# A post-norm attention and feed-forward layer: no setup stage, channel-major input, weights prepared during attention, first norms moved ahead

## The chip, the cores and the metric

The kernel runs on one core of a Trainium2 chip. The metric is the device time of one execution in microseconds, lower is better. TensorE (PE) multiplies, VectorE (DVE), ScalarE (ACT) and GpSimd (POOL) work element by element, and SyncE (SP) issues every DMA here. The engines are ordered by semaphores alone, and each works its own list in order.

## The reference

The input x is 8 x 2048 x 256 in float32. Cut to what matters:

```python
q = x @ q_w.T + q_b
xd = conv1d(x, conv_w, stride 2, padding 1, one filter of 3 per channel) + conv_b
k, v = xd @ k_w.T + k_b, xd @ v_w.T + v_b            # 1024 keys for 2048 queries
a = softmax(q k^T / 4) v                              # 16 heads of 16
x = layernorm(x + a @ out_w.T + out_b)
h = layernorm(x) * gamma + beta
w1, w2 = (fc1_q - 128) * scales1, (fc2_q - 128) * scales2    # int32, scales by rows of 128
y = silu(h @ w1 + b1) @ w2 + b2
out = layernorm(x + x + 0.5 * y)
```

## The kernel before, in words

The 16384 rows are 32 blocks of 512, four for each of 8 batches (`QB`, `NB`, `BPB`). Channels are two chunks of 128 partitions (`CC`). Where accuracy needs it, a float32 value is split into an upper and a lower half (`_hi`, `_lo`), the lower made on GpSimd. Products on float32 tiles issue two PE records each (the order's "x4" is eight records in the trace). The program is four stages, each a block in which all engines start together and end together.

**setup** (L127) loads the int32 weights, the scales and biases. DVE and ACT make w1 and w2 from them, DVE and GpSimd the halves (L228 to L244, L188). PE makes the hidden bias (w1 times beta, L208: 16 products of one column) and the output biases (L203, L214, L215). GpSimd also makes the identity and fills the rows of `k_s` that must be one (L183).

**project** (L252) handles one block after another. PE turns the block of x, loaded by rows, into channels: eight transposes (L348) that ACT copies out (L389). DVE does the convolution (L429 to L437). PE makes q (L359), k (L367), v (L374). ACT copies them out with their biases, and DVE and GpSimd make the halves. SP stores q_hi, q_lo, k_hi, k_lo and v to DRAM (`store`, L299) and loads x for the next batch. v is stored with 16 ones beside the 16 channels of each head (`VC` is 32): with them the weighting also yields the softmax's denominator. At b = 7, keys, values and queries of the first head group are loaded (L332, L333) before the last four stores.

**attention** (L467) has 32 blocks of 32 steps: four groups of four heads (`G`, `HG`), in each eight tiles of 128 keys. In step s PE does the scores of step s + 1 (L602), the products whose maxima are wanted 12 steps later (`first`, L577, `LEAD`), and the weighting of step s (`weigh`, L612). DVE takes the maxima (L683), ACT the exponentials (L658). The maxima of a group are turned by PE (L588) in the fourth step of each group, copied by DVE (L697) and put by SP as one more row into `q_s` (`load_max`, L504). The first score of a group waits for that (L595). SP's list (`one_block`, L515) is in order: in each group `load_max` for the next group, then new q, then the store of o (L535). In the last block of a batch it waits for the group's end, loads its keys and values (`load_kv`, L116) and waits for them to land before q:

```python
sp.wait_ge(pv_done, STEPS * n + KT * (g + 1) + 2)
sp.wait_ge(begun, 1)
load_kv(sp, e, next_kv, g)
sp.wait_ge(kv_loaded[g], KVL * (next_kv + 1))
```

That happens 7 x 4 = 28 times. In the last 12 steps of the last block there are no `first` products. The denominators of blocks 0 to 23 are loaded, inverted (L715) and stored there; `rden_d` is read later.

**finish** (L718) runs in rounds. In round n PE does fc1 of block n (L854), the output projection of block n + 1 (L834), its transposes (L844) and fc2 of block n - 1 (L867). DVE and GpSimd make the norms of block n + 1 (L930 to L946, L1019) and of block n - 2. Rounds -2 and -1 only lead in. The last denominators (blocks 24 to 31) are inverted first of all (L1012).

## Time and profile before

| what | us |
|---|---|
| median of 3 runs (lowest, highest) | 3980.73 (3975.45, 3981.07) |
| the profiled execution, its own time | 3983.98 |
| its span, first to last instruction | 3982.2 |
| PE busy | 3858.0 (97%) |
| PE's weight loads busy | 2013.6 (51%) |
| DVE busy | 3302.4 (83%) |
| ACT busy | 2639.5 (66%) |
| GpSimd busy | 818.9 (21%) |

The span is what lies between the first and the last instruction; the execution's time has 1.8 us more around it. Busy time is an average over stages with different limits, so the table says which engine is filled most and not what a stage waits for. PE's records are pipelined and overlap, so neighbouring starts, not durations, give a product's price.

### The profile page before, as it was taken

The numbers are of one execution on the slowest core, as the hardware profiler recorded it, in microseconds if no ns is written. First come the engines' busy times: TensorE is split into PE (matmuls) and PEld (weight loads), VectorE is DVE, ScalarE is ACT, GpSimd is POOL, SyncE is SP. The second block draws the span as 40 slices with busy tenths as digits, with TensorE's granted clock in tenths as the row PEclk, the third lists the DMA queues.
The fourth block names the chain that finished last, engine by engine and source line by source line (L and its number), as shares of the span: only waits on it lengthen the run. The fifth ranks groups of instructions, "written<-read, shape, count | busy, mean of one in ns | idle before, by whom it ended". The sixth has DMA issues, their size and how long they took to land. (4 is left out here: it accounts for less than half of the span.)

```text
span 3982.2 us, 77196 instructions
## 1 busy us (share of the span) xinstructions
PE 3858.0 (97%) x22952; PEld 2013.6 (51%) x22952; DVE 3302.4 (83%) x4116; ACT 2639.5 (66%) x5028; POOL 818.9 (21%) x535
## 2 busy tenths in 40 slices
PE   7988999999999999999999999999997799999998
PEld 5663333333333333333333333333332689999998
DVE  5658999999999999999999999999993677778775
ACT  3445888888788788888888888887874333433343
POOL 5440000000000000000000000000000677877875
PEclk9997999999999999999999999999997899999999
DMA  7993114112211411311131141122111222222220
GB/s 247 337 329 66 34 33 83 30 33 56 57 33 33 81 33 33 66 47 33 44 70 33 33 82 31 33 55 58 33 38 51 72 73 76 84 79 69 84 83 28
DMA packets 217854, 286.13 MB, mean 72 GB/s; under 512 B 25521, under 2 KB 127921, under 8 KB 217778
## 3 DMA queue, kind: packets, MB, share of 16 engines
q1 hardware_dynamic: 217778, 285.33, 25.7%
q8 instruction: 22, 0.36, 0.0%
q14 instruction: 54, 0.44, 0.0%
HBM read 165.69 MB, written 118.49 MB: 71 GB/s over the span
## 5 line engine op out<-in xcount | busy, mean ns | idle before, releaser
L683 DVE TENSOR_REDUCE half_max<-first_ps 128x2 f32<-128x1024 f32 x2048 | 2413.3, 1221 | 263.3 <-PE first_ps L577 259.2
L658 ACT ACTIVATE probs<-score_ps 128x512 f32<-128x512 f32 x4096 | 2114.9, 603 | 569.5 <-PE score_ps L602 569.4
L602 PE MATMUL score_ps<-q_s,k_s 49*128 49x512 f32 x4096 | 1440.0, 476 | 21.8 <-DMA q_s<-max_row 7.3
L602 PEld LDWEIGHTS score_ps<-q_s,k_s 49*128 49x128 f32 x4096 | 571.7, 185 | 1285.2 <-ACT probs L658 1174.7
L612 PE MATMUL pv_ps<-probs,v_s 128*32 128x512 f32 x8192 | 1099.4, 609 | 0.0
L577 PE MATMUL first_ps<-k_s,q_s 48*128 48x512 f32 x4096 | 905.8, 422 | 20.9 <-PEq L637 12.8
L1042 POOL TENSOR_TENSOR num<-num,rden 128x1024 f32<-128x1024 f32 x32 | 83.8, 2619 | 2784.8 <-DMA rden<-rden_d 2784.8
L899 ACT ACTIVATE act_f<-fc_ps,b 128x512 f32<-128x512 f32 x256 | 175.4, 685 | 454.4 <-PE fc_ps L854 452.3
L577 PEld LDWEIGHTS first_ps<-k_s,q_s 48*128 48x128 f32 x4096 | 402.9, 187 | 73.6 <-DVE half_max L683 18.6
L975 DVE CAST a_hi<-act_f 128x512 fp32r<-128x512 f32 x256 | 251.8, 984 | 142.1 <-ACT act_f L899 141.8
L1023 POOL TENSOR_TENSOR a_lo<-act_f,a_hi 128x512 fp32r<-128x512 f32 x256 | 339.5, 1331 | 79.4 <-DVE a_hi L975 79.4
L867 PE MATMUL fc_ps<-w_hi,a_hi 128*128 128x256 f32 x1024 | 294.4, 287 | 0.9 <-DVE r L961 0.9
L612 PEld LDWEIGHTS pv_ps<-probs,v_s 128*32 128x32 f32 x8192 | 161.7, 108 | 252.1 <-ACT probs L658 149.4
L867 PE MATMUL fc_ps<-w_lo,a_hi 128*128 128x256 f32 x1024 | 286.1, 279 | 0.0
L867 PE MATMUL fc_ps<-w_hi,a_lo 128*128 128x256 f32 x1024 | 286.0, 279 | 0.0
L854 PE MATMUL fc_ps<-h_hi,w_hi 128*128 128x512 f32 x512 | 204.1, 399 | 8.5 <-ACT act_f L899 5.6
L854 PE MATMUL fc_ps<-h_lo,w_hi 128*128 128x512 f32 x512 | 203.5, 398 | 0.0
L854 PE MATMUL fc_ps<-h_hi,w_lo 128*128 128x512 f32 x512 | 203.2, 397 | 0.0
L867 PEld LDWEIGHTS fc_ps<-w_hi,a_hi 128*128 128x128 f32 x1024 | 192.3, 188 | 9.0 <-POOL a_lo L1023 1.2
L867 PEld LDWEIGHTS fc_ps<-w_lo,a_hi 128*128 128x128 f32 x1024 | 192.2, 188 | 7.4
L867 PEld LDWEIGHTS fc_ps<-w_hi,a_lo 128*128 128x128 f32 x1024 | 192.0, 188 | 0.0
L834 PE MATMUL proj_ps<-wo,num 128*128 128x256 f32 x512 | 118.8, 386 | 20.8 <-POOL num L1042 20.8
(83 smaller groups left out, 2427.8 us busy)
## 6 DMA issues: line engine op xcount, KB each, us to landing
q_s<-q_hi_d SPq DMA_DIRECT2D x512, 64.0 KB, 2.1
o_d<-o_sb SPq DMA_DIRECT2D x128, 256.0 KB, 2.1
x_in<-x_in SPq DMA_DIRECT2D x32, 512.0 KB, 5.2
q_hi_d<-q_hi SPq DMA_DIRECT2D x32, 512.0 KB, 3.4
q_lo_d<-q_lo SPq DMA_DIRECT2D x32, 512.0 KB, 4.2
v_d<-v_f SPq DMA_DIRECT2D x32, 512.0 KB, 4.5
k_s<-k_hi_d SPq DMA_DIRECT2D x128, 128.0 KB, 4.2
v_s<-v_d SPq DMA_DIRECT2D x32, 512.0 KB, 6.4
```

Of the source, the lines that this page charges most:

```text
L577: done = pe.matmul(first_ps[keys][:, h, :], q_s[g][at, a, t * P:(t + 1) * P], k_s[g][at, a, keys * 512:(keys + 1) * 512], start=True, stop ...
L602: pe.matmul(bank(s, u)[:, :], k_s[g][at, a, t * P:(t + 1) * P], q_s[g][at, a, :], start=True, stop=True).then_inc(scored, 1)
L612: last = pe.matmul(pv_ps[h * VC:(h + 1) * VC, :], v_s[g][:, t, h, :], probs[s % 2][:, h, :], start=t == 0, stop=t == KT - 1)
L658: nc.scalar.activation(probs[s % 2][:, u, :], bank(s, u)[:, :], ACT.Exp).then_inc(exped, 1)
L683: dve.reduce_max(half_max[g % 2][:, :, a * TT + t, keys], first_ps[keys][:, :, :], AX.X)\
L834: last = pe.matmul(proj_ps[t // 2][:, t % 2, :], num[j][:, c, t * P:(t + 1) * P], wo[:, c, :], start=c == 0, stop=c == CC - 1)
L854: last = pe.matmul(fc1_ps[f % 2][:, :], w[:, c, cut], h[:, c, :], start=i == 0, stop=i == len(pairs) - 1)
L867: last = pe.matmul(fc2_ps[t // 2][:, t % 2, :], a[j][:, f, cut], w[:, f, :], start=f == 0 and i == 0, stop=f == FC - 1 and i == 2)
L899: nc.scalar.activation(act_f[f % RING][:, :], fc1_ps[f % 2][:, :], ACT.Silu, bias=b1[:, f:f + 1]).then_inc(act_up, 1)
L975: dve.tensor_copy(a_hi[j][:, f, :], act_f[f % RING][:, :]).then_inc(ahi_up, 1)
L1023: pool.tensor_tensor(a_lo[j][:, f, :], act_f[f % RING][:, :], a_hi[j][:, f, :].bitcast(F32), ALU.subtract)\
L1042: pool.tensor_tensor(num[j][:, :, :], num[j][:, :, :], rden[j][:, :, :], ALU.mult).then_inc(attn_up, 1)
```

## The change

There is no setup stage. `project` takes x a second time as an argument laid out by channel (`x_c`, made outside the measured time) and loads `x_t` from it, so the transposes and their copies go. The q and k banks are doubled. v is stored without the ones, by partition (`v_d`), and `load_kv` puts its 16 channels of a head beside ones that DVE has written once into `v_s`. The constants and the output biases are made in `project`: before the first block on GpSimd and DVE, behind the last v product on PE. The w1 and w2 weights are made by GpSimd in attention from one pair of buffers, first w1 (`load_w1` behind the first of the last four stores), then w2 (`load_w2` on SP at attention's start, once w1 is done). `load_max(0, 0)` is issued behind group 1's loads instead of behind group 3's. In the last block PE gets `hidden_bias` behind step 21 and the output projection of block 0 (`first_rows`) behind steps 27 to 30. The norms, transposes and halves of block 0 follow behind attention's own work, so `finish` begins with round 0. The last denominators are inverted behind the second round.

```diff
-    v_d = scratch("v_d", [B, NK, H * VC])
+    v_d = scratch("v_d", [B, P, G, KT * HG * D])
+    x_cols = x_c.rearrange("b (c p) n -> b p c n", p=P)
...
-    vs = e["v_d"][b].rearrange("(t p) c -> p t c", p=P)[:, :, g * HG * VC:(g + 1) * HG * VC]
-    sp.dma_start(e["v_s"][g][:, :, :, :].rearrange("p t h c -> p t (h c)"), vs).then_inc(e["kv_loaded"][g], 16)
+    vs = e["v_d"][b][:, g, :].rearrange("p (a d) -> p a d", d=D)
+    sp.dma_start(e["v_s"][g][:, :, :, :].rearrange("p t h c -> p (t h) c")[:, :, 0:D], vs).then_inc(e["kv_loaded"][g], 16)
+
...
+def load_w1(sp, e):
+
+    sp.dma_start(e["w_int"][:, :, :], e["w1_q"].rearrange("(a p) n -> p a n", p=P)).then_inc(e["w_loaded"], 16)
+    for c in range(CC):
+        scales = e["rows"][:, S1_R + c * F:S1_R + (c + 1) * F]
+        sp.dma_start(e["w_s"][:, c, :], scales.to_broadcast([P, F])).then_inc(e["w_loaded"], 16)
+
+
+def load_w2(sp, e):
+
+    sp.dma_start(e["w_int"][:, :, :].rearrange("p c n -> p (c n)").rearrange("p (a n) -> p a n", n=C),
+                 e["w2_q"].rearrange("(a p) n -> p a n", p=P)).then_inc(e["w_loaded"], 16)
+    for c in range(CC):
+        scales = e["rows"][:, S2_R + c * F:S2_R + (c + 1) * F]
+        sp.dma_start(e["w_s"][:, c, :], scales.to_broadcast([P, F])).then_inc(e["w_loaded"], 16)
...
             def load(b, j):
-                sp.dma_start(x_in[j][:, :, :], x_blk[BPB * b + j]).then_inc(x_loaded[j], 16)
...
-                sp.dma_start(by_row(v_d[b][keys, :]), v_f[i][:, :, :, :].rearrange("p t h c -> p t (h c)"))\
-                    .then_inc(stored[i], 16)
+                tiles = slice(j * KB // P * HG * D, (j + 1) * KB // P * HG * D)
+                sp.dma_start(v_d[b][:, :, tiles], v_f[i][:, :, :, :].rearrange("p g t x -> p g (t x)")).then_inc(stored[i], 16)
...
-            for j in range(BPB):
+            by_row = lambda a: a.rearrange("(a p) n -> p a n", p=P)
+            load(0, 0)
+            sp.dma_start(col[:, :], e["cols"]).then_inc(col_loaded, 16)
+            for name in ("wq", "wk", "wv"):
+                sp.dma_start(e[name][:, :, :], by_row(e[name + "_t"])).then_inc(wqkv_loaded, 16)
+            for j in range(1, BPB):
                 load(0, j)
+            sp.dma_start(row[:, :], e["rows"][:, 0:S1_R]).then_inc(ob_loaded, 16)
+            sp.dma_start(wo[:, :, :], by_row(e["wo_t"])).then_inc(ob_loaded, 16)
...
-                    sp.wait_ge(turned, CC * (BPB * b + j + 1))
+                    m = BPB * b + j
+
+                    sp.wait_ge(q_mm, 1 + CC * m + 2 * CC)
+                    sp.wait_ge(begun, 1)
+                    sp.wait_ge(conv_up, 1 + CU * m + (2 * CU if j + 1 < BPB else CU))
                     sp.wait_ge(begun, 1)
                     load(b + 1, j)
                     store(b, j)
 
...
+            sp.wait_ge(ones_up, G)
+            sp.wait_ge(masked, 2 + 2 * G)
             load_kv(sp, e, 0, 0)
             load_q(sp, e, 0, 0)
             for j in range(BPB):
                 store(B - 1, j)
+                if j == 0:
+                    load_w1(sp, e)
...
         def _(pe):
-            def turn(b, j):
-
-                m, i = BPB * b + j, j % 2
-                pe.wait_ge(x_loaded[j % BPB], 16 * (b + j // BPB + 1))
-                for c in range(CC):
-                    pe.wait_ge(xt_up, CC * m + c + 1)
-                    for t in range(TT):
-                        last = pe.transpose(xt_ps[c][:, t * P:(t + 1) * P], x_in[j % BPB][:, t, c * P:(c + 1) * P],
-                                            ident[:, :])
-                    last.then_inc(turned, 1)
...
-                        last = pe.matmul(q_ps[h][:, :], wq[:, c, h * P:(h + 1) * P], x_t[i][:, c, 1:QB + 1],
+                        last = pe.matmul(q_ps[i][h][:, :], wq[:, c, h * P:(h + 1) * P], x_t[j][:, c, :],
...
-            turn(0, 0)
-            each_block(pe, turn, products)
+            pe.wait_ge(wqkv_loaded, 3 * 16)
+            each_block(pe, products)
+
+            pe.wait_ge(consts, 3)
+            pe.wait_ge(ob_loaded, 2 * 16)
+            pe.matmul(bias_ps[:, 1, :], half[:, :], row[:, B2_R:B2_R + C], start=True, stop=True).then_inc(bias_up, 1)
+            pe.wait_ge(vb_up, CC)
+            for c in range(CC):
+                pe.matmul(bias_ps[:, 0, :], vb_wide[:, c, :], wo[:, c, :], start=c == 0, stop=False)
+            pe.matmul(bias_ps[:, 0, :], ones[0:1, :], row[:, OB_R:OB_R + C], start=False, stop=True).then_inc(bias_up, 1)
...
-                dve.wait_ge(conv_up, 1 + CC * m)
-                if j % BPB == 0:
-                    dve.memset(x_t[i][:, :, 0:1], 0.0).then_inc(edge_up, 1)
-                else:
-                    dve.tensor_copy(x_t[i][:, :, 0:1], x_t[1 - i][:, :, QB:QB + 1]).then_inc(edge_up, 1)
-                dve.wait_ge(edge_up, 1 + m + 1)
+                dve.wait_ge(conv_up, 1 + CU * m)
...
+                    dve.scalar_tensor_tensor(out=conv[i][:, c, 1:KB], in0=x_t[j][:, c, 1:QB - 1:2], scalar=w(c, 0),
+                                             in1=acc[1][:, c, 1:KB], op0=ALU.mult, op1=ALU.add).then_inc(conv_up, 1)
+
+                    if j == 0:
+                        dve.tensor_copy(conv[i][:, c, 0:1], acc[1][:, c, 0:1]).then_inc(conv_up, 1)
+                    else:
+                        dve.scalar_tensor_tensor(out=conv[i][:, c, 0:1], in0=x_t[j - 1][:, c, QB - 1:QB],
+                                                 scalar=w(c, 0), in1=acc[1][:, c, 0:1], op0=ALU.mult, op1=ALU.add)\
+                            .then_inc(conv_up, 1)
...
+            for g in range(G):
+                dve.memset(v_s[g][:, :, :, :], 1.0).then_inc(ones_up, 1)
+            dve.wait_ge(col_loaded, 16)
+            dve.tensor_scalar(qb_scaled[:, :], col[:, QB_C:QB_C + CC], float(D) ** -0.5, None, ALU.mult).then_inc(qb_up, 1)
+            dve.wait_ge(consts, 3)
+            for c in range(CC):
+                dve.tensor_scalar(vb_wide[:, c, :], ones[:, :], col[:, VB_C + c:VB_C + c + 1], None,
+                                  ALU.mult).then_inc(vb_up, 1)
             convolve(0, 0)
```

Attention, SP and PE:

```diff
+                    if not refill and g == G - 2:
+
+                        sp.wait_ge(rden_up, 1)
+                        sp.dma_start(all_rdens[0], dens[0][:, :]).then_inc(rden_stored, 16)
+                        sp.wait_ge(rden_stored, 16)
+                        for i in two:
+                            load_rden(sp, e, i, i)
...
             for g in groups[1:]:
                 load_kv(sp, e, 0, g)
                 load_q(sp, e, 0, g)
-            load_max(0, 0)
+                if g == 1:
+                    load_max(0, 0)
+            sp.wait_ge(w_used, 1)
+            load_w2(sp, e)
             with sp.Fori(0, B - 1) as b:
                 for j in range(BPB):
...
+            for i in two:
+                load_rows(sp, e, i, i)
...
+            def first_rows(t):
+
+                if t == 0:
+                    pe.wait_ge(attn_up, 1)
+                    pe.wait_ge(first_used, FIRSTS + 1)
+                for c in range(CC):
+                    last = pe.matmul(first_ps[0][:, t // 2, t % 2 * C:(t % 2 + 1) * C], num[0][:, c, t * P:(t + 1) * P],
+                                     wo[:, c, :], start=c == 0, stop=c == CC - 1)
...
+            def hidden_bias():
+
+                pe.wait_ge(w_used, 1)
+                pe.wait_ge(first_used, FIRSTS + 2)
+                for f in range(FC):
+                    for c in range(CC):
+                        last = pe.matmul(first_ps[1][:, 0, f:f + 1], w1_f[:, c, f * P:(f + 1) * P],
+                                         col[:, BE_C + c:BE_C + c + 1], start=c == 0, stop=c == CC - 1)
+                last.then_inc(b1_mm, 1)
...
+                    if not more and s == STEPS - LEAD + 1:
+                        hidden_bias()
+                    if not more and ROWS_AT <= s < ROWS_AT + TT:
+                        first_rows(s - ROWS_AT)
```

Attention, DVE and GpSimd (the block 0 work on DVE follows `finish`'s own norms, L927 to L947 before, line by line), and the finish:

```diff
+            dve.wait_ge(b1_mm, 1)
+            dve.tensor_tensor(b1[:, :], first_ps[1][:, 0, 0:FC], col[:, B1_C:B1_C + FC], ALU.add)
+
+            dve.wait_ge(xob_up, 1)
+            for a in two:
+                dve.wait_ge(proj_mm, a + 1)
+                dve.tensor_tensor(r1[:, 2 * a:2 * a + 2, :], first_ps[0][:, a, :].rearrange("p (t c) -> p t c", c=C),
+                                  x_res[0][:, 2 * a:2 * a + 2, :], ALU.add).then_inc(r1_up, 1)
+            dve.wait_ge(r1_up, 1 + 2)
+            first_statistics(0, r1)
+            dve.wait_ge(pw[0], 1)
...
+            pool.wait_ge(w_loaded, 3 * 16)
+            for c in range(CC):
+                pool.tensor_scalar(w1_f[:, c, :], w_int[:, c, :], -128.0, 1.0, ALU.add, ALU.mult).then_inc(w_up, 1)
+            for c in range(CC):
+                pool.wait_ge(w_up, c + 1)
+                pool.tensor_tensor(w1_f[:, c, :], w1_f[:, c, :], w_s[:, c, :], ALU.mult).then_inc(w_up, 1)
+            for c in range(CC):
+                pool.wait_ge(w_up, CC + c + 1)
+                pool.tensor_tensor(w_s[:, c, :], w1_f[:, c, :], col[:, GA_C + c:GA_C + c + 1].to_broadcast([P, F]),
+                                   ALU.mult).then_inc(w_up, 1)
+            for c in range(CC):
+                pool.wait_ge(w_up, 2 * CC + c + 1)
+                pool.tensor_copy(w1_hi[:, c, :], w_s[:, c, :]).then_inc(w_up, 1)
+            for c in range(CC):
+                pool.wait_ge(w_up, 3 * CC + c + 1)
+                pool.tensor_tensor(w1_lo[:, c, :], w_s[:, c, :], w1_hi[:, c, :].bitcast(F32), ALU.subtract).then_inc(w_up, 1)
+            pool.wait_ge(w_up, 5 * CC)
+            pool.sem_inc(w_used, 1)
...
+            for j in two:
+                pool.wait_ge(in_loaded[j], LD)
+                pool.tensor_tensor(num[j][:, :, :], num[j][:, :, :], rden[j][:, :, :], ALU.mult).then_inc(attn_up, 1)
+                pool.tensor_tensor(x_res[j][:, :, :], x_res[j][:, :, :], ob[:, :, :], ALU.add).then_inc(xob_up, 1)
...
-            sp.sem_inc(fc2_mm, 3)
-            for j in two:
-                load(j, j)
-
             sp.dma_start(dens[:, :], all_dens[DEN - 1]).then_inc(den_loaded, 16)
-            sp.wait_ge(rden_up, 1)
-            sp.dma_start(all_rdens[DEN - 1], rdens[:, :]).then_inc(rden_stored, 16)
-            sp.wait_ge(rden_stored, 16)
-            rounds(sp, body)
+
+            def last_rden():
+                sp.wait_ge(rden_up, 1)
+                sp.dma_start(all_rdens[DEN - 1], dens[:, :]).then_inc(rden_stored, 16)
+                sp.wait_ge(rden_stored, 16)
+
+            rounds(sp, body, last_rden)
```

PE in a block of the projections (`xt_ps` are the transposes, `q_ps`, `k_ps`, `v_ps` the products). Before:

```order
L346 ISA
L348 MATMUL xt_ps<-ident,x_in 128x128 x4
L346 REGISTER_ALU
L348 MATMUL xt_ps<-ident,x_in 128x128 x4
L355 REGISTER_ALU
L359 MATMUL q_ps<-x_t,wq 128x512 x4
L363 REGISTER_ALU
L367 MATMUL k_ps<-conv,wk 128x256 x4
L374 MATMUL v_ps<-wv,conv 128x256 x4
```

After:

```order
L291 ISA
L293 MATMUL q_ps_0<-x_t,wq 128x512 x2
L291 REGISTER_ALU
L293 MATMUL q_ps_1<-x_t,wq 128x512 x2
L297 ISA
L301 MATMUL k_ps<-conv,wk 128x256 x4
L305 REGISTER_ALU
L308 MATMUL v_ps<-wv,conv 128x256 x4
```

The eight transposes are gone, and the twelve products stand as they did.

SP at attention's start (`k_s`, `v_s`, `q_s` of a group, `max_row` its maxima). Before, from group 3's values on:

```order
L124 DMA v_s<-v_d 128x8x128
L113 DMA q_s<-q_hi_d 16x2x512 x2
L113 DMA q_s<-q_lo_d 16x2x512
L113 DMA q_s<-q_hi_d 16x2x512 x2
L113 DMA q_s<-q_lo_d 16x2x512
L512 DMA q_s<-max_row 1x8x128 x2
L544 UNCONDITIONAL_BRANCH
```

After, from group 1's values on:

```order
L142 DMA v_s<-v_d 128x32x16
L131 DMA q_s<-q_hi_d 16x2x512 x2
L131 DMA q_s<-q_lo_d 16x2x512
L131 DMA q_s<-q_hi_d 16x2x512 x2
L131 DMA q_s<-q_lo_d 16x2x512
L486 DMA q_s<-max_row 1x8x128 x2
L140 DMA k_s<-k_hi_d 16x2x1024
L140 DMA k_s<-k_lo_d 16x2x1024
```

The maxima's row is ahead of groups 2 and 3, and `v_s` is written in 32 pieces of 16 elements per partition instead of 8 of 128.

PE at attention's end (`score_ps` and `pv_ps` are attention's own). Before:

```order
L602 MATMUL score_ps<-q_s,k_s 128x512 x4
L612 MATMUL pv_ps<-probs,v_s 32x512 x8
L471 UNCONDITIONAL_BRANCH
L827 UNCONDITIONAL_BRANCH
L834 MATMUL proj_ps<-wo,num 128x256 x8
L844 MATMUL ht_ps<-ident,hid 128x128 x8
L854 MATMUL fc_ps<-h_hi,w_hi 128x512
```

After, steps 30 and 31:

```order
L588 MATMUL score_ps<-q_s,k_s 128x512 x4
L598 MATMUL pv_ps<-probs,v_s 32x512 x4
L608 MATMUL first_ps<-wo,num 128x256 x2
L598 MATMUL pv_ps<-probs,v_s 32x512 x4
L629 MATMUL first_ps<-ident,hid 128x128 x8
L441 UNCONDITIONAL_BRANCH
L918 UNCONDITIONAL_BRANCH
L945 MATMUL fc_ps<-h_hi,w_hi 128x512
```

The projection of block 0 has gone in front of the stage's end in four pieces of two, of which the last stands here, and its transposes behind the last weighting.

## Rows read from the trace of the kernel before

**Rows 1.** The page's groups: count | busy us, mean ns | idle before, releaser

```profile
L683 DVE TENSOR_REDUCE half_max<-first_ps 128x2 f32<-128x1024 f32 x2048 | 2413.3, 1221 | 263.3 <-PE first_ps L577 259.2
...
L1042 POOL TENSOR_TENSOR num<-num,rden 128x1024 f32<-128x1024 f32 x32 | 83.8, 2619 | 2784.8 <-DMA rden<-rden_d 2784.8
```

**Rows 2.** Windows: length, busy us by engine, PE clock, DMA share, GB/s

```profile
60.00:255.00 195.00, 195.00 (x806) 135.21 (x805) 120.37 (x226) 95.19 (x175) 90.64 (x50) 1.00 1.00 338
```

**Rows 3.** Timeline of PE, projections: start us, us, engine, line, operation

```profile
47.03 1.04 PE L348 MATMUL xt_ps<-ident,x_in 128*128 128x128 f32 x8
47.91 3.60 PE L359 MATMUL q_ps<-x_t,wq 128*128 128x512 f32 x8
...
54.80 1.04 PE L348 MATMUL xt_ps<-ident,x_in 128*128 128x128 f32 x8
```

**Rows 4.** Timeline of setup and the first block

```profile
1.86 15.24 POOL L183 MEMSET k_s<- 32x2048 f32 x8
...
43.58 1.89 PE L367 MATMUL k_ps<-conv,wk 128*128 128x256 f32 x8
```

**Rows 5.** DMA view of 264 to 300 us

```profile
DMA packets 7570, 10.86 MB, mean 302 GB/s; under 512 B 567, under 2 KB 3842, under 8 KB 7570
```

**Rows 6.** Timeline at attention's start

```profile
299.88 1.22 PE L577 MATMUL first_ps<-k_s,q_s 48*128 48x512 f32 x4 [12.82 <-PEq L637]
...
333.16 1.22 PE L602 MATMUL score_ps<-q_s,k_s 49*128 49x512 f32 x3 [6.21 <-DMA q_s<-max_row]
```

**Rows 7.** Timeline of one reload: SP's issues, then PE's scores

```profile
615.47 0.40 SPq L124 DMA_DIRECT2D v_s<-v_d  x1
622.01 0.80 SPq L113 DMA_DIRECT2D q_s<-q_hi_d  x2
...
624.93 0.38 SPq L535 DMA_DIRECT2D o_d<-o_sb  x1
626.17 1.36 SPq L512 DMA_DIRECT2D q_s<-max_row  x2
...
630.85 0.50 PE L602 MATMUL score_ps<-q_s,k_s 49*128 49x512 f32 x2
```

**Rows 8.** The page's DMA issues: KB each, median us from issue to landing

```profile
o_d<-o_sb SPq DMA_DIRECT2D x128, 256.0 KB, 2.1
```

**Rows 9.** DMA view of 1.78 to 2.0 us, while `col` lands

```profile
DMA packets 83, 0.01 MB, mean 37 GB/s; under 512 B 83, under 2 KB 83, under 8 KB 83
...
q1 hardware_dynamic: 83, 0.01, 37.9%
```

**Rows 10.** Windows, while the 512 B packets of `v_s` land

```profile
619.80:620.80 1.00, 1.00 (x14) 0.50 (x7) 0.93 (x1) 0.46 (x2) 0.00 (x0) 1.00 1.15 289
```

**Rows 11.** Windows of line L208 alone, in setup

```profile
13.60:20.40 6.80, 6.79 (x32) 6.79 (x32) 1.00 0.54 189
```

**Rows 12.** Windows, attention's last steps

```profile
3029.30:3053.40 24.10, 22.18 (x73) 5.69 (x72) 0.00 (x0) 11.80 (x24) 0.00 (x0) 0.50 0.01 2
```

**Rows 13.** Timeline of attention's end and the finish's head

```profile
3018.23 9.75 DVE L715 RECIPROCAL rdens<-dens 128x512 f32<-128x512 f32 x3
...
3054.03 3.64 PE L612 MATMUL pv_ps<-probs,v_s 128*32 128x512 f32 x16
...
3064.12 0.39 SPq L794 DMA_DIRECT2D x_res<-x_in  x1
...
3078.49 5.63 PE L834 MATMUL proj_ps<-wo,num 128*128 128x256 f32 x16 [20.81 <-POOL num L1042]
...
3087.75 1.22 DVE L953 TENSOR_TENSOR r<-proj_ps,x_res 128x512 f32<-128x512 f32 x2
...
3089.01 1.40 DVE L930 BATCH_NORM_STATS2 stats<-r 128x6 f32<-128x256 f32 x4
...
3104.83 0.79 PE L854 MATMUL fc_ps<-h_hi,w_hi 128*128 128x512 f32 x1 [1.41 <-DVE h_lo L967]
```

**Rows 14.** The chain of waits at the finish's head: start us, us, what

```profile
3071.18 13.28 DMA last_dens<-o_d
```

575 lines of the change are left out of this document (286 added, 289 removed).

## The prediction, before the change was run

> **What bounds the kernel now.** I cut the span by its stages first: setup until 31 us, projections until 300, attention until 3058, then the finish. In attention the profile's costliest group on DVE, the reductions over `first_ps`, has a mean of 1221 ns and waits for PE, while GpSimd sits idle for 2784.8 us before its first real work of the finish [rows 1]. That long middle is hardly touched by the change: what it can win lies at the three seams, setup to projections, projections to attention, attention to finish, and in the projection loop.
>
> In the projections the windows view has PE busy without a gap, and the DMA engines too: share 1.00 at 338 GB/s [rows 2]. Two resources are at their limit together. The timeline of PE gives the block's period: transposes start at 47.03 and again at 54.80, 7.77 us, and the eight transposes take 47.03 to 47.91, 0.88 us [rows 3].
>
> **The setup stage goes.** Before, GpSimd fills `k_s` with ones from 1.86 to 17.1, and the first `k_ps` product comes at 43.58 [rows 4]. After, x (512 KB) and wq, wk, wv are in front on SP's queue: 1.28 MB at the 338 GB/s of [rows 2] is 3.8 us and a few for issue and landing, so q can begin at about 7. But the first convolution is behind four memsets of `v_s`, `qb_scaled` and `vb_wide` on DVE, which wait for the column load and share those first 17 us with GpSimd's fills. I put the first `k_ps` at 17, the fills' end, with 12 and 23 as ends (q's 6.9 us at the low clock behind 7, less what overlaps; the fills' end plus some six DVE operations): 43.6 - 17 = 26.6 us gained (20 to 31).
>
> **The transposes and bytes of each block go.** PE's block is 7.77 - 0.88 = 6.89 us. The bytes of a block are now 512 KB each for x, q_hi, q_lo and v and 256 KB each for k_hi and k_lo, 2.62 MB; v without its ones halves, leaving 2.36 MB, and at 338 GB/s that takes 6.98 us. So DMA would be the bound by a hair; x goes from 1 KB to 2 KB runs, v's store from 2 KB to 512 B runs. I take 6.98, a gain of 0.79 us per block, for the 28 blocks before the first `load_kv`: 22.1 us (ends 0 if DMA doesn't get faster, 28 x 0.88 = 25).
>
> **The end of the projections gets fuller.** From that `load_kv` at 264 to 300 the queues move 10.86 MB [rows 5], and attention's first product is at 299.88 [rows 6]. It now moves 4 x 0.26 MB less of v stores and 0.26 MB less of `v_s`, but 2.1 MB of `w1_q` and scales more (`load_w1`, in front of three of the four last stores): +0.8 MB, 2.4 us lost at 338 GB/s (0 to 6, if all of `w1` adds). The output biases, four products and two copies that setup had, now stand behind the last v product, hidden by the last stores, which end some 12 us later; without that cover they would cost about 4.
>
> **Attention's start.** PE has finished the twelve parts ahead and waits 6.21 us for `max_row` to land behind the loads of groups 2 and 3 [rows 6]. `load_max(0, 0)` now goes before them. I count 5.8 us gained (0 to 6.2). Those loads are then issued some 12 us later, and are first wanted at step 4 and step 12. SP then waits for `w_used`: ten GpSimd operations of 1024 columns. GpSimd's product of that size takes 2619 ns [rows 1], so 26 us, while SP comes to the wait some 36 us after the stage's start. What hides all 18 operations is GpSimd's idle 2785 us; were `w1` later than that, `load_max(0, 1)` would be late and PE would stand at step 8.
>
> **The reload of keys and values.** 28 times in attention SP issues the keys, `v_s` and, once they have landed, q, o and the next `max_row`. Before: `v_s` is issued at 615.47, landed when q is issued at 622.01, o is issued by 625.3, both rows of `max_row` from 626.17 to 627.5, and PE scores with them at 630.85 [rows 7]. So SP has 0.85 us of air, and `max_row`, with o's 2.1 us to landing [rows 8], 1.2 more: 2.0 in all. The change cuts `v_s` from 1024 runs of 512 B to 4096 runs of 64 B (its shape goes from 128x8x128 to 128x32x16). The cost of such a packet isn't in this trace; bounds are the 104 B packets of `col`: 37.9% of 16 engines in 0.22 us for 83 packets, 16 ns each [rows 9]; and the 512 B packets of `v_s`: share 1.15 at 289 GB/s, 33 ns each [rows 10]. 4096 packets over 16 engines take 4.1 us by the first and 8.4 by the second, where 1024 of 33 ns take 2.1. I take the first, being nearest in size: 2.0 us later, just inside the air, cost 0. The other end is 6.3 - 2.0 = 4.3 us, 28 times: 120 us.
>
> **Additions in attention's last steps.** `hidden_bias` puts 16 products of one column, 32 records, behind step 21, ahead of everything that follows on PE. The same in setup took 6.79 us for 32 records [rows 11]; the transposes, as many weights each, take 0.88 / 8 = 0.11 each in [rows 3], which makes 3.5. The clock is still full at step 21: 3.5 (to 6.8). `first_rows` adds 16 records after steps 27 to 30. There the granted clock is 0.50, 1.2 GHz, and PE is busy 22.18 of 24.10 us [rows 12], so it has little room. In the finish such 16 take 5.63 us behind an idle stretch [rows 13]: 5.6. The ends are 3.4 at the full clock (the 6.89 us without transposes in [rows 3] hold 8192 columns in 24 records, so 256 take 0.215) and 6.9 at half. Together 9.1 us lost. ACT and DVE have room there, and the weighted products end later by that sum.
>
> **The head of the finish shrinks.** The weighted products end at 3057.67, and the first `fc_ps` product starts at 3104.83, 47.2 us later [rows 13]. In between lie the end of the stage, ten loads, GpSimd's product, then `last_dens`, 13.28 us of the chain [rows 14], whose reciprocal stands in DVE's queue in front of `r1`, and only then the norms. After the change what is left behind PE is the chain from the second half of `first_rows`, which ends some 1.8 us (one of the two steps of 3.64) before PE's end. From there: half of 1.22 for `r1`; from the statistics at 3089.01 to the first `fc_ps` 15.8; and the meeting of the engines between stages, which no row isolates: between 0 and the 6.5 us from PE's end to the finish's first load (3064.12), in which a copy and stores also lie; I take 1. That is -1.8 + 0.6 + 15.8 + 1 = 15.6 us, a gain of 31.6 (26 to 33). `last_dens` moves behind the second round and is wanted at block 24. The finish's rounds themselves are the same.
>
> **The sum.** -26.6 - 22.1 + 2.4 - 5.8 + 9.1 - 31.6 = -74.6 us. Against the profiled execution's 3983.98 us: 3909.4. That execution lies 3 us above the median of the runs (3980.73) and I forecast 3909.
>
> **Rivals.**
> (a) *The short runs of `v_s` stall PE.* By the 33 ns end, each reload is 4.3 us late: 28 x 4.3 = 120, 3984 - 75 + 120 = 4029 us, slower than before. It decides from 2.0 us on; at 4.7 us later per reload (packets of 26 ns) all gains are gone. For it: SP's air is small and its queue in order. Against: the 104 B rows. Chance 0.12, with 0.06 for slower than before and the rest for a part of it (3930 to 3970). The Trainium skill's page DMA: Bandwidth & Descriptors (Specifications) wants 512 B or more for line rate, "below this, SDMA does read-modify-write", and so speaks against this load. The 104 B rows don't show such a price, on 83 packets.
> (b) *The projections stay at DMA's pace.* If engines with share 1.00 gain nothing from fewer bytes, since the count of packets stays as it was, the 22.1 us are gone: 3931. For: the full share. Against: the engines were only as busy as PE let them be, since the period was PE's sum. Chance 0.13.
> (c) *GpSimd's weights slow DVE.* 18 operations of about 2.6 us are 47 us; were DVE's reductions blocked for all of it, attention would be up to 47 us longer, 3956. Against: they read PSUM alone. The Trainium skill's page SBUF — State Buffer tells of an exclusive lock on the shared ports only for DVE operations in a two-port mode or with two SBUF inputs; no row here shows GpSimd beside these reductions. Chance 0.06.
> (d) *The head doesn't shrink.* If the denominators' path (reciprocals, a store, `load_rden`) comes late, `first_rows` waits on PE and the 31.6 are lost: 3941. Against: the reciprocals end at 3028 [rows 13], and `first_rows` stands behind step 27, four cold steps before PE's end. Chance 0.04.
>
> **The numbers.** The forecast holds with 0.65, between 3893 and 3925 by the ends of its own terms (12 us less for a quicker start and a higher clock in the tail, 16 more). Adding (b) and part of (a) and (d) makes the range 3892 to 3944. About 0.2% is what a measurement of this kernel can tell from no change. Faster: 0.65 + 0.13 + 0.06 + 0.04 + 0.04 (part of (a)) = 0.92; same 0.02; slower 0.06.
>
> **What would show it.** Right: first `k_ps` near 17; period of `q_ps` 6.9 to 7.0; no wait for `max_row` at the start; q issued at most 8.5 us after `v_s`, and the waits of `score_ps` for `q_s` near 0; the last steps about 9 us longer; `fc_ps` some 15 us behind the last weighted product. Wrong: a period of 7.7 (b), waits for `max_row` at every reload (a), reductions above 1221 ns in the first 60 us (c), or PE waiting in front of `first_rows` (d).

## The result, and the profile after

| | before | after |
|---|---|---|
| median of 4 runs each | 3980.9 us | 3952.7 us |
| lowest to highest | 3975.5 to 3981.3 | 3949.5 to 3953.0 |
| profiled execution (span) | 3984.0 (3982.2) | 3952.9 (3951.1) |

The ratio is 0.993, interval 0.9913 to 0.9948: 28 us faster, by the two profiled executions 31.1. Forecast were 74.6 us and 3909, in a range of 3892 to 3944. The sign was right, the size was not, and the time lies outside the range.

Where the time went is read from seven moments that both traces have. Three of them, the weighted products of steps 0, 32 and 992 of attention's 1024, stand in PE's timelines of after and of before:

```profile
285.91 1.08 PE L598 MATMUL pv_ps<-probs,v_s 128*32 128x512 f32 x4
...
382.68 1.06 PE L598 MATMUL pv_ps<-probs,v_s 128*32 128x512 f32 x8
...
2948.53 1.07 PE L598 MATMUL pv_ps<-probs,v_s 128*32 128x512 f32 x8
```
```profile
337.68 1.08 PE L612 MATMUL pv_ps<-probs,v_s 128*32 128x512 f32 x4
...
423.65 1.07 PE L612 MATMUL pv_ps<-probs,v_s 128*32 128x512 f32 x8
...
2962.72 1.07 PE L612 MATMUL pv_ps<-probs,v_s 128*32 128x512 f32 x8
```

| stretch | before us | after us | gained | forecast |
|---|---|---|---|---|
| to the first `k_ps` product | 43.58 | 14.98 | 28.6 | 26.6 |
| to attention's first product | 256.30 | 239.71 | 16.6 | 19.7 |
| to the first weighted product | 37.80 | 31.22 | 6.6 | 5.8 |
| to step 32 | 85.97 | 96.77 | -10.8 | 0 |
| steps 32 to 992 | 2539.07 | 2565.85 | -26.8 | 0 |
| to the end of the last weighted product | 94.95 | 104.68 | -9.7 | -9.1 |
| to the first `fc_ps` product | 47.16 | 16.26 | 30.9 | 31.6 |
| to the end | 877.37 | 881.63 | -4.3 | 0 |

Five of the stretches came out within 4 us of the forecast. Of the 43.5 us missing, 41.9 lie in the three that it set to nothing.

**The projections**, as forecast, keep PE busy in every period. Windows of after, and its PE timeline (columns as in [rows 2] and [rows 3]):

```profile
60.00:230.00 170.00, 170.00 (x592) 112.10 (x590) 150.98 (x239) 73.88 (x125) 89.91 (x48) 1.00 1.02 334
```
```profile
14.98 1.89 PE L301 MATMUL k_ps<-conv,wk 128*128 128x256 f32 x8
...
18.43 3.60 PE L293 MATMUL q_ps<-x_t,wq 128*128 128x512 f32 x8
...
25.32 1.02 PE L293 MATMUL q_ps<-x_t,wq 128*128 128x512 f32 x2
```

DMA moves 334 GB/s here, and a block takes 25.32 - 18.43 = 6.89 us, where [rows 3] had 7.77. At the end more is lost. PE's timeline of after, and one row of before:

```profile
231.62 1.99 PE L308 MATMUL v_ps<-wv,conv 128*128 128x256 f32 x8 [1.27 <-ACT v_f L339]
...
254.69 1.22 PE L563 MATMUL first_ps<-k_s,q_s 48*128 48x512 f32 x4 [18.77 <-PEq L657]
```
```profile
285.17 1.89 PE L374 MATMUL v_ps<-wv,conv 128*128 128x256 f32 x8
```

PE has multiplied the last v at 233.6 and attention begins 21.1 us later. Before, it was 287.06 to 299.88 [rows 6], 12.8 us.

**Attention's start.** `max_row` of group 0 now goes ahead of groups 2 and 3, and the wait of 6.21 us [rows 6] is gone. The next wait is longer. SP's timeline of after, then PE's:

```profile
276.41 1.54 SPq L486 DMA_DIRECT2D q_s<-max_row  x2
...
292.83 7.77 SPq L131 DMA_DIRECT2D q_s<-q_hi_d  x2
...
304.43 0.42 SPq L171 DMA_DIRECT2D w_int<-w_q_in  x1
...
306.24 1.35 SPq L486 DMA_DIRECT2D q_s<-max_row  x2
```
```profile
313.57 0.90 PE L588 MATMUL score_ps<-q_s,k_s 49*128 49x512 f32 x2 [8.12 <-DMA q_s<-max_row]
```

Two issues of `q_s`, right behind a load of `v_s`, take 7.77 us (6.38 behind that of group 2): SP stands at the issue. Then w2 (2 MB) goes out, and `max_row` of group 1 behind it, at 306.24. PE starts with it at 313.57, 8.12 us after it was ready to. SP came to `w_used` 50 us behind the stage's start, where the prediction had 36, and GpSimd was not what it waited for: the first ten operations had ended at 271.2.

**The reload**, at the turn from one batch to the next. SP's timeline of after, then PE's, then SP's of before, then the window of after:

```profile
638.09 0.40 SPq L142 DMA_DIRECT2D v_s<-v_d  x1
646.25 0.78 SPq L131 DMA_DIRECT2D q_s<-q_hi_d  x2
...
649.17 0.37 SPq L516 DMA_DIRECT2D o_d<-o_sb  x1
652.60 1.40 SPq L486 DMA_DIRECT2D q_s<-max_row  x2
```
```profile
655.26 0.90 PE L588 MATMUL score_ps<-q_s,k_s 49*128 49x512 f32 x2 [1.72 <-DMA q_s<-max_row]
```
```profile
688.28 0.37 SPq L535 DMA_DIRECT2D o_d<-o_sb  x1
691.69 1.39 SPq L512 DMA_DIRECT2D q_s<-max_row  x2
```
```profile
653.00:664.00 11.00, 9.28 (x44) 3.98 (x38) 5.72 (x5) 5.22 (x10) 0.00 (x0) 0.60 0.21 61
```

`v_s` takes longer to land, as forecast. The view of that tile in after gives min, median and max; [rows 7] had 622.01 - 615.47 = 6.5 from issue to what waits for it, and here it is 8.2:

```profile
DMA to landing us min/median/max: 7.7/8.4/10.3
```

But behind o's store SP needs 3.06 us until it issues the next `max_row` (649.54 to 652.60), and so it did before (3.04, 688.65 to 691.69), where the three groups ahead of it needed 0.8 to 1.1. Its row had been copied at 648.8, and between the two issues SP's loop over the batches turns. [rows 7], which I took for all 28 reloads, is one of group 0, where nothing turns. At the turn there was no air. PE stands 1.72 us, and then the granted clock falls: 0.60 on average in these 11 us, 1.00 in the 11 us ahead of them. The seven waits of the profile:

```profile
PE score_ps L588 <- DMA q_s<-max_row: 20.1, 7, 8.1
```

One is the 8.12 us at the start, the other six the six turns of SP's loop. By the 128 steps around them they cost 2.2 to 5.7 us each (340.7 to 344.2 for the 338.5 of before). 2 of it are the wait; five of the six are followed by 6.8 to 10.2 us at 1.2 GHz, and the sixth, which cost 2.2, by none. How much it comes to differs from execution to execution: 18 to 27 us for the six together, in six traces whose program is the same there (after, e2, e5, e6, e7, e9).

**The tail and the head.** PE's timeline of after:

```profile
3006.41 3.73 PE L619 MATMUL first_ps<-col,w_f 128*128 128x1 f32 x32
...
3052.15 1.06 PE L598 MATMUL pv_ps<-probs,v_s 128*32 128x512 f32 x8
3065.40 1.94 PE L629 MATMUL first_ps<-ident,hid 128*128 128x128 f32 x8 [12.19 <-ACT hid L698]
3069.47 0.76 PE L945 MATMUL fc_ps<-h_hi,w_hi 128*128 128x512 f32 x1 [2.13 <-ACTq L1015]
```

`fc_ps` starts 16.3 us behind the end of the last weighted product; 15.6 was forecast.

**The reductions** of [rows 1] still have a mean of 1221 ns on the page of after.

**The finish.** PE's timelines, first `fc_ps` products of two blocks, after and before:

```profile
3124.34 0.39 PE L945 MATMUL fc_ps<-h_hi,w_hi 128*128 128x512 f32 x1
...
3905.74 0.39 PE L945 MATMUL fc_ps<-h_hi,w_hi 128*128 128x512 f32 x1
```
```profile
3159.03 0.40 PE L854 MATMUL fc_ps<-h_hi,w_hi 128*128 128x512 f32 x1
...
3937.39 0.40 PE L854 MATMUL fc_ps<-h_hi,w_hi 128*128 128x512 f32 x1
```

They are 29 blocks apart: 26.94 us per block after and 26.84 before. No instruction of these rounds was changed.

### The profile page after: what moved, and what is told of

It is laid out like the page before. It is cut to its first block and busy times, and to the rows that moved or that the text cites. A ratio compares the mean times of both kernels' runs of the same rounds, so it can differ in the third digit from the quotient of the medians.

```text
span 3951.1 us, 76505 instructions
## 1 busy us (share of the span) xinstructions
PE 3847.0 (97%) x22696; PEld 1997.0 (51%) x22696; DVE 3336.2 (84%) x4142; ACT 2612.8 (66%) x4968; POOL 840.7 (21%) x547
## 5 line engine op out<-in xcount | busy, mean ns | idle before, releaser
L711 DVE TENSOR_REDUCE half_max<-first_ps 128x2 f32<-128x1024 f32 x2048 | 2413.5, 1221 | 290.8 <-PE first_ps L563 287.1
L563 PE MATMUL first_ps<-k_s,q_s 48*128 48x512 f32 x4096 | 912.0, 423 | 26.8 <-PEq L657 18.8
L817 POOL TENSOR_TENSOR num<-num,rden 128x1024 f32<-128x1024 f32 x2 | 4.7, 2356 | 2687.2 <-DMA rden<-rden_d 2687.2
L563 PEld LDWEIGHTS first_ps<-k_s,q_s 48*128 48x128 f32 x4096 | 412.4, 189 | 79.9 <-issue 20.0
L1069 DVE CAST a_hi<-act_f 128x512 fp32r<-128x512 f32 x256 | 243.6, 952 | 146.0 <-ACT act_f L992 144.9
L1117 POOL TENSOR_TENSOR rstd<-var_e,minus_half 128x4 f32<-128x4 f32 x94 | 99.4, 1057 | 133.9 <-DVE var_e L1029 133.8
```

What stands on the lines that cost most here:

```text
L563: done = pe.matmul(first_ps[keys][:, h, :], q_s[g][at, a, t * P:(t + 1) * P], k_s[g][at, a, keys * 512:(keys + 1) * 512], start=True, stop ...
L711: dve.reduce_max(half_max[g % 2][:, :, a * TT + t, keys], first_ps[keys][:, :, :], AX.X)\
L1069: dve.tensor_copy(a_hi[j][:, f, :], act_f[f % RING][:, :]).then_inc(ahi_up, 1)
L1117: pool.tensor_tensor(rstd[k][:, :], var_e[k][:, :], minus_half[:, :], ALU.pow).then_inc(pw[k], 1)
```

## The experiments

The kernel before ran again beside them and had medians of 3977.1 (e1 to e4), 3980.3 (e5 to e8), 3979.0 (e9 to e11) and 3973.9 us (e12), so ratios are the safer comparison; the changed kernel's is 0.993. "First block" is the span between the first weighted products of steps 0 and 32, "last block" that from step 992 to the end of the last weighted product (104.7 us after). The intervals of e2, e6, e7 and e9 touch or overlap the changed kernel's (0.9913 to 0.9948), so for these four the reading rests on the stretches of the trace and not on the time.

### The turn of the batch: e1, e4, e3

e1 moves one load in SP's program:

```diff
 def one_block(n, refill, next_kv):
     for g in groups:
-        if g + 1 < G: load_max(n, g + 1)
+        if 0 < g < G - 1: load_max(n, g + 1)
...
+    if refill: load_max(n + 1, 1)
```

> The changed kernel with one thing moved: SP loads the max_row of group 1 of the next block at the end of a block, in front of the turn of its loop, where it had done so behind the turn. The short runs of v_s stay. Theory A (each new batch of keys costs some 5 us because three things add up on SP: 2 us more for v_s to land, the 3.04 us between o's store and the next max_row in which the loop turns, and then a wait of PE of 1.7 to 2 us that drops the clock to 1.2 GHz for 6.8 to 10.2 us): the six waits at steps 134, 262, ..., 774 go, 26.6 us, 3952.7 - 26.6 = 3926 us, within 3 us, with no interval of clock 0.50 between 330 and 3000 us. Rival B (the short packets alone keep max_row from landing in time, or the clock falls for another reason and the waits follow from it): the waits stay, 3952 us.

Measured: 3924.1 us (3920.8 to 3926.1), 0.9869 (0.9853 to 0.9886). SP's timeline, then PE's waits:

```profile
649.52 0.37 SPq L516 DMA_DIRECT2D o_d<-o_sb  x1
650.07 1.37 SPq L486 DMA_DIRECT2D q_s<-max_row  x2
```
```profile
PE score_ps L591 <- DMA q_s<-max_row: 9.4, 1, 9.4
```

`max_row` follows o's store after 0.2 us, one wait of the seven is left (that at the start), and 128 steps take 338.6 us everywhere, where after had up to 344.2. The clock shows no low stretch between 319 and 2981 us. This is theory A: at the reloads the short runs alone stall nothing. Nor does the turn alone: before, with runs of 512 B, PE waited three times for `max_row`, 7.3 us in all with the 6.21 of the start.

e4 keeps the turn where it is and takes `v_s` out of the chain: `load_kv` loads keys alone, and in the reload SP loads `v_s` behind the next `max_row`:

```diff
-    sp.dma_start(e["v_s"][g]..., vs).then_inc(e["kv_loaded"][g], 16)
+    sp.dma_start(e["v_s"][g]..., vs).then_inc(e["v_loaded"][g], 16)
...
+        if next_kv is not None and g > 0: load_v(sp, e, next_kv, g - 1)
```

> The changed kernel with the load of v_s taken out of the chain: keys are loaded and waited for, then q, o's store and max_row, and v_s (still 4096 runs of 64 B) comes behind the next max_row with a semaphore of its own; it is wanted 14 steps later. Theory A: SP has some 4 us of air at every reload, no PE wait for max_row at the batch turns, 3926 us, within 4 us (the start of attention may shift by a few us, since v_s of group 3 comes behind max_row of group 1 there). Rival B (the DMA engines' time for short packets delays max_row wherever they stand): waits stay in part, 3940 to 3955 us.

Measured: 3918.2 us (3915.3 to 3924.7), 0.9861 (0.9845 to 0.9877), and no wait for `max_row` at all. SP's timeline, at the turn and at attention's start:

```profile
637.67 0.38 SPq L530 DMA_DIRECT2D o_d<-o_sb  x1
641.25 1.38 SPq L496 DMA_DIRECT2D q_s<-max_row  x2
642.85 0.41 SPq L147 DMA_DIRECT2D v_s<-v_d  x1
644.29 3.50 SPq L132 DMA_DIRECT2D q_s<-q_hi_d  x2
```
```profile
294.46 0.42 SPq L176 DMA_DIRECT2D w_int<-w_q_in  x1
...
301.86 1.34 SPq L496 DMA_DIRECT2D q_s<-max_row  x2
```

From o's store to the next `max_row` SP still needs 3.2 us (638.05 to 641.25), now with room. The issue behind `v_s` still takes 3.50 for two, where two take 0.8 elsewhere. The time is 8 us under theory A's 3926, and that is the first block: 88.8 us for 96.8. w2 is still ahead of `max_row` there, but `v_s` of group 3 no longer stands in front of w2, so w2 goes out 10 us earlier, 7.4 us ahead of `max_row` instead of 1.8, and PE does not wait. In e3 too, w2 is where it was, the first block is 87.4 us, and PE does not wait there.

e3 gives v its old layout, with the ones stored and loaded:

```diff
-v_f = [sb(f"v_f{i}", [P, G, KB // P, HG * D]) for i in two]
+v_f = [sb(f"v_f{i}", [P, KB // P, H, VC]) for i in two]
...
-vs = e["v_d"][b][:, g, :].rearrange("p (a d) -> p a d", d=D)
+vs = e["v_d"][b].rearrange("(t p) c -> p t c", p=P)[:, :, g * HG * VC:(g + 1) * HG * VC]
```

> The changed kernel with v as it was before: v is stored with its halves of ones and v_s loaded in 1024 runs of 512 B instead of 4096 of 64 B. Theory A: no PE wait for max_row at the six batch turns, period of a batch 338.4 us instead of 343.6, 26.6 us less; no SP issue of over 5 us at attention's start. Against it stands what the smaller v saved in the projections: blocks of 2.62 MB in 6.89 us would be 380 GB/s, and if DMA gives only 338 GB/s the block's period goes from 6.89 to 7.75, 28 x 0.86 = 24 us lost. Sum 3952.7 - 26.6 - 5 (start) + 24 = 3945 us. Rival B: boundaries as they are, 3970 us. Rival E (DMA was never a bound in the projections): period 6.89, 3921 us.

Measured: 3925.6 us (3920.0 to 3930.2), 0.9875 (0.9858 to 0.9893). A window of it:

```profile
60.00:120.00 60.00, 60.00 (x208) 39.31 (x207) 53.39 (x84) 25.68 (x45) 30.82 (x17) 1.00 1.02 364
```

The waits at the turns go here too (two of 0.4 us are left, and the clock does not fall behind them). In the projections the period is neither 7.75 nor 6.89 throughout. 2.62 MB per 6.89 us would be 380 GB/s. The DMA engines move 364, more than the 338 of [rows 2], and fall behind slowly: sixteen periods are 6.89 us, the later ones up to 7.61. Attention starts 7.4 us later than in the changed kernel, not 24. So the smaller v did save time in the projections, and lost more of it at the reloads.

### Attention's start: e2

```diff
-sp.wait_ge(w_used, 1)
-load_w2(sp, e)
 with sp.Fori(0, B - 1) as b:
...
+sp.wait_ge(w_used, 1)
+load_w2(sp, e)
```

> The changed kernel with one thing moved: the load of w2 and its scales (2 MB, with SP's wait for w_used in front) comes behind the loop over the batches, no longer in front of max_row of group 1. Theory C (PE's wait of 8.1 us at 305.4 is for max_row behind these 2 MB in the DMA queues): max_row is issued at some 304.4, 1.8 us earlier, and lands 3 to 4 us later instead of 7.3; PE waits some 2.4 us, so 5.7 us less, and with a shorter stretch of low clock 3952.7 - 6 to 8 = 3946 us. Rival D (the loads of v_s of groups 2 and 3, whose 4096 short packets each block SP's next issue for 6.4 and 7.8 us, are what is late, and the DMA engines still work them off): max_row lands only as early as it is issued, 1.8 us, 3951 us.

Measured: 3947.4 us (3941.8 to 3953.3), 0.993 (0.9913 to 0.9948), and in the profiled execution 3945.8 for 3952.9. The first block takes 88.7 us for 96.8, and PE no longer waits for `max_row` there: SP issues it at 302.79. The wait has moved along with the load:

```profile
2690.10 0.40 SPq L171 DMA_DIRECT2D w_int<-w_q_in  x1
...
2691.80 1.36 SPq L486 DMA_DIRECT2D q_s<-max_row  x2
```
```profile
2699.50 0.90 PE L588 MATMUL score_ps<-q_s,k_s 49*128 49x512 f32 x2 [6.08 <-DMA q_s<-max_row]
```

Here too 2 MB stand 1.7 us ahead of a `max_row`, and PE waits 6.08 us. The 128 steps around it take 349.2 us for 338.4, so the move lost 10.8 us there and won 8.0 in the first block; that this execution is 7 us shorter all the same comes from its turns (18 us for 27), which the edit does not touch. Theory C holds for a `max_row` that is issued 1.7 or 1.8 us behind w2. It is not the whole cause at the start: e3 and e4 are rid of the wait with w2 in its place, so the 8.12 us took both, the 2 MB and the 7.77 us for which SP had stood behind `v_s`.

### The end of the projections: e5

e5 takes w1 from between the last stores and puts both weight loads behind o's stores of the last batch, w1 in its second block and w2 in its third:

```diff
 for j in range(BPB):
     store(B - 1, j)
-    if j == 0:
-        load_w1(sp, e)
```

> The changed kernel with both weight loads moved: w1 and its scales (2 MB) no longer stand between the last stores of the projections but behind o's store of the last batch's second block, w2 (2 MB) one block later. Theory F (the projections end late because w1's 2 MB are ahead of the last stores: 2.1 MB at 338 GB/s is 6.2 us): attention's first product 6 us earlier, at 248.5 instead of 254.7. At attention's start as in the kernel with w2 alone moved (first block 8 us shorter). 3952.7 - 6 - 8 = 3939 us. Rival G (the last stores are late because SP stood 5.4 us at the issue of q behind the short runs of v_s, and DVE waits for the stores of the block before): first product unchanged at 254, 3945 us.

Measured: 3932.0 us (3929.1 to 3935.5), 0.9884 (0.986 to 0.9907). PE's timeline of it, and of e8 (below), where `v_s` of group 0 also goes behind the last stores:

```profile
247.77 1.22 PE L564 MATMUL first_ps<-k_s,q_s 48*128 48x512 f32 x4 [12.33 <-PEq L658]
```
```profile
243.11 1.22 PE L580 MATMUL first_ps<-k_s,q_s 48*128 48x512 f32 x4 [8.89 <-PEq L674]
```

254.69 becomes 247.77, so w1 cost 6.9 us, and then 243.11: the short runs of `v_s`, behind which two issues stood for 4.7 us, cost 4.7 more. F and G are both right, in sequence. Neither weight load stalls PE now. The time is 7 us under the 3939 of theory F; 4 of it lie in the last block, which no edit of e5 touches (next section).

### Hidden bias in the tail: e6, e9

> The changed kernel with 14 of the 16 products of hidden_bias left out (seven of the eight columns of the hidden bias are not computed). Those 32 records lie at 3006.41 to 3010.14, 3.7 us, in the changed kernel's trace. If PE's order is the price, as forecast, the last block is 3.3 us shorter and the time 3949 us; if the stretch is bound by ACT's exponentials and the products only fill gaps, 3952 us.

Measured: 3940.2 us (3937.6 to 3942.9), 0.9904 (0.9875 to 0.9934). The kernel leaves out seven of the eight columns of the hidden bias. The last block is 96.4 us, not 104.7: 8.3 us shorter for 3.3 us of products. The low stretch of the clock, which began right behind them (3010.4) and lasted 37.5 us in the changed kernel, lasts 23.9. In e1 it begins inside them, and 32 records of one column then take 5.58 us:

```profile
2979.92 5.58 PE L622 MATMUL first_ps<-col,w_f 128*128 128x1 f32 x32
```

e9 moves them instead:

```diff
-        if not more and s == STEPS - LEAD + 1:
-            hidden_bias()
...
 one_block(NB - 1, False)
+hidden_bias()
 first_hidden()
```

> The changed kernel with hidden_bias moved: PE multiplies its 16 products behind the last weighted products, where it waits 12.2 us for hid, and no longer behind step 21; DVE adds b1 behind the second statistics. If the 3.7 us of hidden_bias were path in the last block and the wait for hid covers them, the last block is 3.7 us shorter and the head (16.8 us from the last weighted product to the first fc1 product) stays: 3949 us, and a few us less if the stretch of low clock also gets shorter (from 37.5 us, as it did to 23.9 when the products were left out). If the head is bound by PE's queue after all, it grows by 3.7 us and the time stays at 3952.7 us.

Measured: 3938.7 us (3928.5 to 3942.6), 0.99 (0.9878 to 0.9922). PE's timeline:

```profile
3037.94 3.73 PE L619 MATMUL first_ps<-col,w_f 128*128 128x1 f32 x32
```

The last block is 94.9 us, 9.8 less than after, and from its end to `fc_ps` it stays 16.3 us: PE's wait for `hid` covers them. The low stretch is 20.5 us.

One pair of traces is not enough here, for the last block differs between executions of the same text: it is 100.7 us in e5 and in e7, which change nothing in it. The eight traces that have the products behind step 21 (after, e1 to e5, e7, e8) give 100.7 to 105.2 us with a low stretch of 27.3 to 37.5; the four that do not (e6, e9, e10, e11) give 93.7 to 96.4 with 17.1 to 23.9. The groups do not overlap, and their means are 7.5 us apart. So the 16 products cost about 7.5 us there, twice the forecast's 3.5, and the part beyond their own 3.7 goes with a longer stretch at 1.2 GHz. Why it is longer is not shown: it begins 59 to 65 us behind step 992 with and without them.

### The finish: e7, e11, e12

e7 is one line in `finish`:

```diff
+pad = sb("pad", [P, 112])
 a_hi = [sb(f"a_hi{i}", [P, FC, QB], F32R) for i in two]
```

> The changed kernel with 448 bytes of nothing allocated in front of the finish's activations, so that a_hi, a_lo and what follows lie at the same place modulo 1 KB as in the kernel before (they had moved by 576 bytes). In all variants of the changed kernel so far a block of the finish takes 26.94 us, in the kernel before 26.84, all of it in fc2's products (283 against 279 ns). If the place in SBUF makes that, the period goes back to 26.84 and the time to 3949.7 us; if it is the program (its length, its place in memory, its semaphores), 26.94 and 3952.7 us.

Measured: 3944.1 us (3943.1 to 3945.0), 0.9914 (0.9885 to 0.9943). That is 8.6 us less where 3 were expected. In the profiled execution the finish is 2.6 us shorter, as expected; 4.0 are the last block and 2.2 the turns, which the edit does not touch.

> The kernel before, with nothing changed but 576 bytes of nothing in front of the finish's activations, which puts a_hi and a_lo where the changed kernel has them (512 bytes past a multiple of 1 KB instead of 960). If the place of these tiles makes fc2's pace, a block of the finish goes from 26.84 to 26.94 us, fc2's products from 279 to 283 ns, and the time 3 us up, to 3984 us; if something else of the changed program made it, 26.84 us and 3981 us.

Measured: 3982.4 us against 3973.9, 1.002 (1.0007 to 1.0034): slower, by 3 to 14 us, where 3 were expected. One group of each page, of before, after, e7 and e12 in this order (busy us, mean ns of one):

```profile
L867 PE MATMUL fc_ps<-w_hi,a_lo 128*128 128x256 f32 x1024 | 286.0, 279 | 0.0
```
```profile
L958 PE MATMUL fc_ps<-w_hi,a_lo 128*128 128x256 f32 x1024 | 289.6, 283 | 0.0
```
```profile
L959 PE MATMUL fc_ps<-w_hi,a_lo 128*128 128x256 f32 x1024 | 286.0, 279 | 0.0
```
```profile
L868 PE MATMUL fc_ps<-w_hi,a_lo 128*128 128x256 f32 x1024 | 289.6, 283 | 0.0
```

279 ns where `a_hi` begins 960 bytes past a multiple of 1 KB, 283 at 512 past, in either program; a block takes 26.84 and 26.94 us. The place in SBUF alone makes it. `a_hi` and `a_lo` are what these products load as weights, and the pages have the weight load too at 188 ns before and in e7, and at 191 after and in e12. e11 is e10 (below) with 512 bytes for 448, which puts the tiles at the multiple itself:

> The same with 512 bytes in front of the activations in place of 448, so that a_hi and a_lo begin at a multiple of 1 KB, where they began at 960 bytes past one (26.84 us per block) or 512 past one (26.94). If what counts is that they don't begin at 512 past one, 26.84 us and 3898 us; if 1 KB multiples are worse, as two tiles read together often would be, 26.9 us or more and 3901 us.

Measured: 3896.1 us (3894.6 to 3897.6), 0.9797 (0.9775 to 0.9819), 26.94 us per block, 283 ns. So 0 and 512 are slow and 960 is fast; what the rule is stays open, and no run shows anything of two tiles that are read together.

### All together: e8, e10

e8 is e4 and e5 together, with `v_s` of group 0 behind the last stores, those of groups 1 and 2 behind the loads of group 3, and group 2's keys and q ahead of the first `max_row`.

> All that paid, together: v_s out of the chain of the reload, both weight loads in the last batch's blocks, v_s of group 0 behind the last stores of the projections, keys and q of group 2 ahead of the first max_row. By theories A, C and F: 3918.2 (v_s out of the chain) - 6 (w1) - 3 (no 2 MB ahead of max_row at step 8) - up to 5 (SP no longer stands behind v_s at 216 us) = 3906 us, within 5 us. If G is right and F wrong, the first product still comes 5 us earlier, by v_s of group 0, and the time is 3911 us.

Measured: 3904.8 us (3899.2 to 3906.4), 0.9814 (0.9794 to 0.9834). The first block takes 85.7 us.

> The kernel of the last call with everything that paid (3904.8 us), with the 448 bytes in front of the activations and with hidden_bias in PE's wait: 3904.8 - 2.9 (period of a finish block 26.84 for 26.94) - 3.7 = 3898 us, within 3 us.

Measured: 3890.4 us (3888.7 to 3892.9), 0.9783 (0.9768 to 0.9798), 8 us under the forecast. The last block is 93.7 us for e8's 102.2, which is 4.8 of these 8; the rest no trace shows (by the profiled executions e10 lies 8.8 us under e8, by the medians 14.4). This is the best version: 62 us below the changed kernel and 2.2% below the kernel before.

## Why the prediction was wrong

- **Setup goes**: 28.6 us for 26.6. The size is right, the path is not: the forecast had GpSimd's fills as the end, at 17. After, the first q product waits until 9.49 for `wv` to land, q takes 5.5 us and `k_ps` follows it at 14.98 without a gap, while the fills run until 16.8.
- **The loop**: 0.88 per block for 0.79. PE, not DMA, is the bound; 338 GB/s was what PE asked for, and e3 shows 364. Rival (b) is out.
- **The end of the projections**: -8.0 for -2.4 (16.6 less 28 blocks of 0.88), beyond the end of 6. This term was too small. w1's 2 MB cost 6.9 us (e5), and what was missing is SP's issue behind short runs, 4.7 more (e8). Together they lose 11.6, and the 1.3 MB that the sum took off win 3.9 by its 338 GB/s: -7.7, near the measured -8.0.
- **Attention's start**: this step failed. The wait for `max_row` of group 0 went as forecast (6.6 for 5.8). For the next one the prediction had PE stand at step 8 only if `w1` were late. PE stood there, 8.12 us, though `w1` was done at 271.2: SP was late by its stands behind `v_s` (6.38 and 7.77 us), and so w2's 2 MB went out 1.8 us ahead of `max_row`. The first block lost 10.8 us; taking away either of the two gives back 8 to 9 of it (e2, e4, e3).
- **The reload**: the step that failed most, 26.8 us. The delay of `v_s` was right, 2 us. The air of 2.0 us was read at one of four groups and multiplied by 28; the group at whose end SP's loop turns has 2.2 us less (3.04 for 0.85), and so none. So rival (a) holds at 6 of 28 reloads, with 2.2 to 5.7 us each for a wait of 2, since behind five of them the clock falls. (a)'s range for a part of it, 3930 to 3970, holds the result. The Trainium skill (DMA: Bandwidth & Descriptors, Specifications) wants runs of 512 B for line rate. The trace agrees as far as it goes: half the bytes in 64 B runs land 2 us later.
- **The tail**: -9.7 for -9.1, and that is luck. `hidden_bias` is worth about 7.5 where 3.5 stood (e6, e9 and the eight traces with it), and the records of `first_rows` take 6.9 us where 5.6 stood. The sum came out by the clock of the kernel before: it fell 62 us behind step 992 in both, but before it stayed low for 58.0 us, after for 37.5, until two steps from the end. In e12, whose attention is that of the kernel before, it stayed low for 34.1 us, and the last block took 86.2 us instead of 95.0. Against that trace the tail lost 18.5 us, not 9.7.
- **The head**: 30.9 for 31.6. Right; (d) is out.
- **The finish**: -4.3 for 0, of which about 3 by the tiles' place in SBUF (32 blocks of 0.10; e7 gives back 2.6). The cause of the other 1 stays open.
- **Rival (c)**: no sign of it; the reductions keep 1221 ns.

The parts add up in e10. Against the changed kernel its first product of attention comes 12.1 us earlier, the first block is 9.2 us shorter, steps 32 to 992 are 27.3, the last block 10.9 and the finish 2.9: 62.4 of the 62.5 us between the two profiled executions.

## What to carry over

A slack that is read at one place of a loop holds for that place: look for the iteration at which the queue's own loop turns, or at which a weight load stands ahead, before multiplying. A bulk load in the same queues costs whoever is issued right behind it: where a row of maxima was issued 1.7 or 1.8 us behind 2 MB, PE waited 6 to 8 us for it, and where it was 7.4 us behind, not at all. So put it behind a store with 10 us of nothing after it, as e5 does. A wait of 2 us on TensorE cost up to 5.7 here, since the steps behind it run at 1.2 GHz. And where the clock falls at the end of a stage, one pair of traces does not measure that end: it differed by 9 us between two traces of the same text.
